# Causal attention with exact maxima and a routed feed-forward: products of 64-row head pairs, two-bank maxima, two PSUM rings and a planned TensorE order

## The reference

```
h = layernorm(x) * (1 + ca) + sa
q, k, v = h @ Wq, h @ Wk, h @ Wv          # 16 heads of 8
q, k = rope(q), rope(k)
scores = q k^T / sqrt(8), causal
x = x + ga * (softmax(scores) v) @ Wo
h = layernorm(x) * (1 + cb) + sb
x = x + gb * moe(h)                       # 8 experts, top 2, capacity 640, gelu, 128 -> 512 -> 128
```

## Time and profile before

| | |
|---|---|
| median of 3 runs | 691.77 us (690.76 to 692.2) |
| span of the profiled execution | 684.6 us; its time outside the span was not recorded, against the median it is 7.2 us |
| TensorE busy | 564.4 us, 82% |
| VectorE busy | 449.5 us, 66% |
| ScalarE busy | 350.3 us, 51% |
| GpSimd busy | 207.4 us, 30% |

### The profile page before, as it was taken

How to read it: one execution, slowest core, us unless ns; L and a number is a source line. 1 busy time by engine, 2 the same in 40 slices (tenths; PEclk the granted TensorE clock), 3 DMA queues, 4 the chain that set the end, 5 groups by cost and what they waited for, 6 DMA issues and landing times.

```text
span 684.6 us, 10732 instructions
## 1 busy us (share of the span) xinstructions
PE 564.4 (82%) x3592; PEld 249.6 (36%) x3592; DVE 449.5 (66%) x1004; ACT 350.3 (51%) x736; POOL 207.4 (30%) x501
## 2 busy tenths in 40 slices
PE   3164878899998999989999999899988841999980
PEld 2042433344332333333333334233321131687770
DVE  3866889698899898989898988898700061112123
ACT  1200424567666765747677767577788710223220
POOL 6203424512314823025202013034020224055461
PEclk9676999999999999999999999999999975799995
DMA  8830805541140611100000000000000002022206
GB/s 192 224 52 3 179 11 139 142 128 38 45 125 13 193 36 44 30 20 29 5 1 3 1 2 1 1 17 17 1 3 1 0 1 70 1 71 64 65 35 192
DMA packets 43523, 37.63 MB, mean 55 GB/s; under 512 B 4880, under 2 KB 39097, under 8 KB 43436
## 3 DMA queue, kind: packets, MB, share of 16 engines
q1 hardware_dynamic: 39312, 30.64, 17.2%
q0 software_dynamic: 2448, 4.63, 1.9%
q10 hardware_dynamic: 1708, 1.67, 1.2%
HBM read 20.39 MB, written 17.05 MB: 55 GB/s over the span
## 4 chain that ended last, share of the span: by engine, by line
PE 59%; DVE 21%; DMA 6%; issue 4%; POOL 4%; ACT 3%; SPq 3%; POOLq 0%; ACTq 0%; DVEq 0%
PE av L1163 17%; PE score L1147 14%; DVE mpart L877 12%; PE work L1125 11%; PE work L1255 6%; PE av L1269 4%; ACT PRB L714 3%; PE work L1128 1%; PE work L1099 1%; SPq L423 1%; DMA k_rows<-part 1%; DMA m_rows<-mrow 1%; PE score L1269 1%; PE work L1188 1%; POOL slots_x L647 1%
## 5 line engine op out<-in xcount | busy, mean ns | idle before, releaser
L714 ACT ACTIVATE PRB<-score 128x512 f32<-128x512 f32 (+3 forms) x640 | 300.8, 540 | 161.8 <-PE score L1147 159.1
L877 DVE TENSOR_REDUCE mpart<-work 128x1 f32<-128x512 f32 (+3 forms) x560 | 339.5, 668 | 58.1 <-PE work L1125 35.0
L1125 PE MATMUL work<-KS,QP 128*128 128x512 bf16 (+3 forms) x640 | 213.0, 356 | 39.0 <-DMA QP<-q_rows 19.2
L1147 PE MATMUL score<-QP,KS 128*128 128x512 bf16 (+3 forms) x640 | 213.5, 353 | 17.4 <-DMA QP<-m_rows 8.1
L1163 PE MATMUL av<-PRB,VX 128*9 128x512 f32 (+3 forms) x1264 | 144.8, 540 | 0.0
L610 POOL TENSOR_SCALAR_AFFINE_SELECT PRB<-PRB 128x128 f32<-128x128 f32 x256 | 70.6, 294 | 176.9 <-ACT PRB L714 174.0
L1147 PEld LDWEIGHTS score<-QP,KS 128*128 128x128 bf16 x640 | 59.1, 98 | 178.1 <-ACT PRB L714 112.3
L1125 PEld LDWEIGHTS work<-KS,QP 128*128 128x128 bf16 x640 | 64.0, 100 | 93.4 <-DVE mpart L877 42.8
L756 ACT ACTIVATE QP<-work 128x640 f32<-128x640 f32 x32 | 22.5, 703 | 72.5 <-PE work L1255 72.5
L660 POOL DMA_INDIRECT parts_y<-KS,back_to x40 | 38.9, 971 | 55.0 <-DVEq L1051 45.0
L1128 PE MATMUL work<-causal,identb 128*128 128x128 bf16 x256 | 51.8, 229 | 0.0
(11 more groups left out here) (163 smaller groups left out, 359.5 us busy)
## 6 DMA issues: line engine op xcount, KB each, us to landing
q_rows<-part SPq DMA_DIRECT2D x24, 128.0 KB, 2.3
KS<-k_rows SPq DMA_DIRECT2D x16, 192.0 KB, 4.7
k_rows<-part SPq DMA_DIRECT2D x21, 128.0 KB, 2.3
slots_x<-RT SPq DMA_DIRECT2D x8, 325.0 KB, 3.6
KS<-slots_x SPq DMA_DIRECT2D x8, 325.0 KB, 3.1
W<-in_L_ffn_c_proj_dram SPq DMA_DIRECT2D x4, 512.0 KB, 5.4
CS<-in_L_ffn_c_fc_dram SPq DMA_DIRECT2D x4, 512.0 KB, 5.5
PRB<-parts_y SPq DMA_DIRECT2D x8, 256.0 KB, 4.2
```

What stands on the lines that cost most here:

```text
L714: a.activation(PRB[:, t % PR, q0:QB], SC[t % 3][:, q0:QB], ACT.Exp, scale=SCALE).then_inc(exped, 1)
L877: v.tensor_reduce(mpart[:, u % 2, cols, k0 // QB], w[:, 0:len(heads) * keys].rearrange("p (j k) -> p j k", k=keys), AX.X, ALU.max).then_in ...
L1125: last = t_.matmul(row, QP[:, h % 2, h // 2, b % 2, (i % TB) * P:(i % TB + 1) * P], KS[:, h // 2, k0:k0 + keys], start=True, stop=not ends)
L1147: t_.matmul(SC[t % 3][:, q0:QB], KS[:, h // 2, kt * P:(kt + 1) * P], QP[:, h % 2, h // 2, b % 2, q0:QB], start=True, stop=True).then_inc(s ...
```

## The change

- Scores and maxima use 64 rows. `QP` has no zeroed copies (half the size, no clearing), and a step does both heads of a pair: one product on rows 0 to 63, one on rows 64 to 127, into two different banks.
- A maxima piece is a pair of heads in two banks (for 128 and 256 keys both pairs), and one reduction reads both banks. The mask is added by two parts for each half, with rows swapped by four small DMAs, so that it too uses 64 rows at a time.
- Two rings in the place of one: `D` with two slots of two banks for what VectorE reads, `A` with the three score banks for what ScalarE reads, scores and other steps alike.
- q and qr become one step of two products and one wide VectorE product, k and kr too; two tiles are normalised by one pair of instructions.
- The order comes from `Planner`, which keeps a clock for each engine with a cost for each step and always takes the step that could start first (priorities break ties). Value products are issued for two key tiles at a time (`AVG`). Block 1 is projected before the first maxima.
- SP follows the same list: expansion at a block's k, the q of blocks 2 and 3 reloaded by SP. `empty`, `XK`, `On` and `OnT` get memory of their own, one of the two `HG` buffers moves to `PRB`.

```diff
-NW = 4
+DW = 2
+AW = 3
+D_KIND = ("mod", "q", "k", "max", "norm", "wo", "logit", "rank", "tail")
+A_KIND = ("xt", "v", "negmax", "ot", "h2t", "score")
...
+GUESS = {"xn": (0.0, 1.0, 0.2), "xt": (0.6, 0.6, 0.1), "q": (1.9, 4.5, 0.1), "k": (1.9, 2.0, 0.1), "v": (1.0, 0.6, 0.1),
...
+         "negmax": (0.2, 0.3, 5.0)}
+NEGATE = 2.5
+LAUNCH_AT = {2: 3, 3: 5}
...
+        self.plan = [("ln", 0), ("xt", 0), ("mod", 0), ("q", 0), ("k", 0), ("ln", 1), ("mod", 1)] + projections(1)[:4]
+        self.plan += [("v", 0), ("v", 1)]
...
+    def piece(self, u, n, at):
+        pairs, i, k0, keys = max_pieces(u)[n]
+        masked = k0 + keys == P * (i + 1)
+        self.d_step(("max", u, n), at, len(pairs) * (keys / 2200 + 0.03 + 0.13 * masked), 0.13 + 2 * len(pairs) * keys / 960)
...
+    def scores(self, u, kt, a, at):
+        wide = QB - first_column(u, kt)
+        self.pe = at + wide / 2200 + 0.04
+        for half in range(2):
+            self.a_bank(0.18 + wide / 1200)
...
+    def avs(self, group, at):
+        self.pe = at + 0.2
+        for u, kt in group:
+            self.pe += (QB - first_column(u, kt)) / 610
...
+                lead = u + n / len(max_pieces(u)) - (scores[0][0] + scores[0][1] / (TB * (units()[scores[0][0]][0] + 1)) if scores else 0)
+                choices.append((self.d_start(), (-1 if lead < LEAD else 2) if self.dve - self.pe < 1.0 else 4, "max", None))
...
+                    waiting = self.a_start(2, ready)
+                    choices.append((waiting, 0 if self.act - self.pe < 0.8 else 3, "score", None))
...
+                    if waiting is not None and waiting < at + long and self.act < at + long + SLACK:
+                        at = max(at, waiting + 0.01)
+                    choices.append((at, 3.5, "av", None))
+            at, _, what, chain = min(choices, key=lambda c: (c[0], c[1]))
...
+AVG = 2
+SLACK = 0.5
+LEAD = 1.5
...
-        QP = sb("QP", [P, 2, NPAIR, 2, QB], bf16)
+        QP = sb("QP", [P, NPAIR, 2, QB], bf16)
...
+            for s in plan:
+                if s[0] == "k":
+                    expand(s[1])
+                    if s[1] == 0:
+                        swap_masks()
+                elif s[0] == "negmax":
+                    put_negmax(s[1])
...
+                        reload_q(b + 2, st.tile[u, kt, GH - 1])
...
+                        v.tensor_reduce(part[:, :, pairs[0], i % TB], w[:, :, 0:keys], AX.X,
+                                        ALU.max).then_inc(slot_free(s), 1)
...
+                        for half in range(2):
+                            rows = slice(64 * half, 64 * half + ROWS)
+                            last = t_.matmul(w[:, half, n * keys:(n + 1) * keys],
+                                             QP[rows, 2 * g + a, b % 2, (i % TB) * P:(i % TB + 1) * P],
+                                             KS[rows, 2 * g + a, k0:k0 + keys], start=True, stop=not ends)
...
+                        for part in range(2 if ends else 0):
+                            for half in range(2):
+                                rows = slice(64 * half, 64 * half + 64)
+                                last = t_.matmul(w[:, half, (n + 1) * keys - P:(n + 1) * keys], mask_i[rows, part, :],
+                                                 mask_c[rows, part, :], start=False, stop=part == 1)
...
+                    banks = [take_bank(s, half) for half in range(2)]
+                    for half, (w, ok) in enumerate(banks):
+                        rows = slice(64 * half, 64 * half + KROWS)
+                        t_.matmul(w[:, q0:QB], KS[rows, 2 * g + a, kt * P:(kt + 1) * P],
+                                  QP[rows, 2 * g + a, b % 2, q0:QB], start=True, stop=True).then_inc(ok, 1)
```

More of the change, by code:

```diff
@@ L186 @@
+AVG = 2
+SLACK = 0.5
+LEAD = 1.5
 class Steps:
     def __init__(self):
-        self.plan = make_plan()
-        self.ring = {s: n for n, s in enumerate(x for x in self.plan if x[0] not in RINGLESS)}
-        self.tile = {}
+        self.plan = Planner().run()
+        self.dring = {s: n for n, s in enumerate(x for x in self.plan if x[0] in D_KIND)}
+        self.aring, self.areads, self.tile, self.diag = {}, {}, {}, {}
+        self.bank_use = []
         for s in self.plan:
-            if s[0] == "score":
-                self.tile[s[1:]] = len(self.tile)
@@ L196, in __init__ @@
-        self.diag = {}
-        for s in self.plan:
-            if s[0] == "score" and s[2] >= TB * units()[s[1]][0]:
-                self.diag[s[1:]] = len(self.diag) + 1
+            if s[0] not in A_KIND:
+                continue
+            self.aring[s] = len(self.bank_use)
+            if s[0] != "score":
+                self.areads[s] = len(self.areads) + 1
+                self.bank_use.append(("read", self.areads[s]))
+                continue
+            _, u, kt, a = s
+            for half in range(2):
+                j = 2 * a + half
+                self.tile[u, kt, j] = len(self.tile)
+                self.bank_use.append(("exp", len(self.tile)))
+                if kt >= TB * units()[u][0]:
+                    self.diag[u, kt, j] = len(self.diag) + 1
@@ L326, in block_kernel @@
         modt_ok, modb_ok = sem("modt_ok"), sem("modb_ok")
-        full = [sem(f"full{i}") for i in range(NW)]
-        free = [sem(f"free{i}") for i in range(NW)]
+        d_full, d_free = [sem(f"d_full{i}") for i in range(DW)], [sem(f"d_free{i}") for i in range(DW)]
+        a_full, a_read = [sem(f"a_full{i}") for i in range(AW)], sem("a_read")
         roped, kparts_ok, qparts_ok = (
@@ L1121, in _ @@
                     ends = k0 + keys == P * (i + 1)
-                    for n, j in enumerate(heads):
-                        h = GH * g + j
-                        row = w[:, n * keys:(n + 1) * keys]
-                        last = t_.matmul(row, QP[:, h % 2, h // 2, b % 2, (i % TB) * P:(i % TB + 1) * P],
-                                         KS[:, h // 2, k0:k0 + keys], start=True, stop=not ends)
-                        if ends:
-                            last = t_.matmul(row[:, keys - P:keys], identb[:, :], causal[:, :],
-                                             start=False, stop=True)
@@ L1240, in turn @@
                 last.then_inc(xbt_ps, 1)
[L1242 to L1243 removed]
+            for r in range(len(dring) - DW, len(dring)):
+                pe.wait_ge(d_free[r % DW], r // DW + 1)
+            for r in range(len(st.bank_use) - AW, len(st.bank_use)):
+                wait_bank(pe, r)
             pe.wait_ge(w1_in, 16 * E // 2)
```

521 lines of the change are left out of this document (291 added, 230 removed).

## The result

The changed kernel takes 801.80 us (median of 4 runs, 799.71 to 803.69) where the kernel before takes 691.26 on the same chip: a ratio of 1.160, 95% interval 1.157 to 1.163. The forecast was 648. The span of the traced execution is 798.0 us, against 684.6 before. In every run where both were recorded, the time is about 2 us more than the span, so the trace of before is of an execution some 5 us faster than its median: marks are compared with it to within 5 us. Where executions of one kernel lie apart, a table's time is the median of all, and the marks are those of the one that was traced.

What follows compares the result with a forecast made beforehand. TensorE bounds the kernel, VectorE close behind; after, VectorE and buffers. Maxima end at 43 + 352 + 44 + 20 = 459, then 45.2, 33.7 and 103.7: span 641.6, plus 7.2 gives 649, rounded to 648; 8-in-10 range 612 to 684.

Steps and rivals of the forecast that it cites:

- Pairs run side by side: TensorE's scores and maxima: a 512-column pair of 64-row products takes 0.25 us, between bounds of 0.22 and 0.43.
- pairs don't overlap: Rival: TensorE's 64-row products run one after the other, its work is 426 us; time 692 to 706, chance 0.08.
- Reductions: VectorE's maxima: 288 two-bank reductions, mean near 1.22 us, sum 309 us by count, near 320 expected in the profile.
- The start: Block 1 projected before the first maxima: first reduction at 43 us instead of 37.7, first score at 67 as now.
- SP's stalls: Maxima rows queue behind block expansions and q reloads in SP's queue: 20 us of VectorE idleness, range 0 to 40.
- The 7.2 us outside the span: Time outside the profiled span, 691.8 - 684.6, added to the forecast span of 641.6.
- each of 80 groups costs VectorE 0.55 us: Each group of value products delays refills, idling VectorE between 0 and 0.8 us; 0.55 taken, 44 us in all.
- 44 + 20: VectorE's idleness until the maxima end: 44 us beside value-product groups plus 20 at SP's queue, 64 in all.
- two key tiles take 4.9 us: ScalarE's exponentials: 3.9 + 1.0 us per two key tiles, exactly the present 2.44 per key tile.
- 45.2 as now: From the end of the maxima to the last value products: 45.2 us, unchanged because the 2.44 us period stays.
- The clock: Rival: TensorE idles enough to fall to 1.2 GHz; with a third of the stage cold, about 700 us, chance 0.04.
- three signs named for being wrong: Pairs starting 0.4 us apart, the lower clock in the stretch, or a few maxima-row stalls of 5 us or more.

Runs made afterwards that it cites:

- e3: The changed kernel with value products in groups of one key tile instead of two, the planner ordering anew: 743.6 us, ratio 1.073.
- e4: The changed kernel, but a score pair computes into its first bank before waiting for the second, instead of claiming both first: 756.6 us, ratio 1.092.
- e5: The changed kernel with both edits, value products in groups of one key tile and a pair's banks claimed one by one: 729.1 us, ratio 1.051.
- e15: The kernel before, old order, with two slots of two banks for all ring steps, two-bank maxima, products still on 128 rows: 713.6 us, ratio 1.039.
- e17: The kernel before, old order, with every single-head score and maxima product, and the masks of those pieces, on 64 rows: 704.1 us, ratio 1.019.
- e2: The changed kernel with one extra 128-row product, later overwritten, before each score pair, after its banks are taken: 883.3 us, ratio 1.275.
- e8: The kernel before, old order, with every single-head score and maxima product on its head's 64 rows, masks still on 128: 721.9 us, ratio 1.041.
- e6: The changed kernel with four narrow products of zeros into the open value bank before each score pair's wait for banks: 782.8 us, ratio 1.129.
- e9: The changed kernel with one extra 64-row product, later overwritten, into a pair's first bank before the wait for the second: 773.5 us, ratio 1.113.
- e14: The changed kernel with value products in groups of one and two extra 64-row products before the wait for a pair's second bank: 750.7 us, ratio 1.094.
- e16: The kernel before, old order, with value products of two key tiles issued together as a group of 16: 692.0 us, ratio 1.002.
- e18: The kernel before, old order, with the edits of e16 and e17 together: 741.9 us, ratio 1.075.
- e11: e5 with SP putting unit 0's maxima row ahead of block 1's expansion: 709.2 and 727.2 us in two executions.
- e12: e5 with the planner's costs for a score's exponential and a reduction set as the trace shows them: 712.0 and 731.1 us in two executions.
- e13: Changed kernel, groups of one, one extra 64-row product before a pair's second-bank wait, maxima rows moved from SP's to GpSimd's queue: 729.0 us, ratio 1.062.

## Why the prediction was wrong

The sizes of the single parts were right. Pairs run side by side: 0.22 us forecast at the lower bound, 0.25 taken, 0.22 measured. The rival "pairs don't overlap" is out. Reductions: 288, mean of the wide ones 1.219 us (1.22 forecast), 322 us in all (320). The start: first reduction at 45.3 (43), first exponential at 73.7 (67 for its score, 72.98 measured). SP's stalls: VectorE idle 13.1 us before 74.2 and 8.7 before 118.4, TensorE's queue standing at a score whose maxima row was late; 22 us, 20 forecast. Epilogue and experts take 3.4 us longer. The 7.2 us outside the span were about 2, the rest being the faster execution that was traced; as before and forecast were treated alike, this does not touch the 648. One sum beside the forecast is off: 0.28 us a pair makes TensorE's work 334 us, not 328.

**The step that each of 80 groups costs VectorE 0.55 us, together 44, failed.** The last maxima row comes at 577, not 459. Of the 118 us, 2 are the later start, 13 VectorE's busy time (364.6 against 352) and 103 idleness: 167 us where the sum had 44 + 20. I had costed a group at 1.83 us, its time at full clock, counted one refill behind it, and let a pair take its banks when they came. In fact the pair's claim needs two of three banks free at once, and the group was 3.5 us long whenever the clock was low. The waits show it: the forecast had VectorE's idleness "in pieces under 1 us", and the largest entry has 47 pieces of 1.6 us in the mean, up to 3.9, such as the 3.14 us behind the group at 395.94. e3, e4 and e5 put 58, 45 and together 73 us on these two grains. e15, at full clock, shows a second term that the sum lacked: the two-bank slots of VectorE's ring, 3.9% by themselves in the old order.

**The step on ScalarE's side, that two key tiles take 4.9 us (the present 2.44 each), failed, and with it "45.2 as now".** It held with banks claimed singly, groups of one and a high clock (2.43 in e5). As changed it is 7.7: 3.5 for a group at the lower clock, 1.44 and twice 1.21 for the pairs (two exponentials need 1.0) and 0.3 to the next group. The tail behind unit 15 is 79.6 us instead of 45.2, of which some 7 are the score work moved behind the mark.

**The clock, a rival at 0.04, was weighed wrongly.** The lower clock was one of the three signs named for being wrong, and it came. I expected TensorE about 80% busy at a clock near 1.00, from a stretch that was 84% busy at 1.00. It was 78% busy and granted 0.81; in the last unit 68% and 0.66; e17 had 92% and 0.90. So one row of 128-row products said little about a mix with 64-row ones and other pauses. It was priced too low as well: about 700 us in the prediction, where the kernel took 802. My own count should have warned: 318 us of work in the 461 from 43 to 504 is 69%, and only busy time, which reads 464 where I counted 420, made it look like 80. With the low clock, TensorE's busy time over the whole stage (45 to 656 us) is 453 us, about what it was (464 from 37.5 to 547). In busy time nearly all that the 64 rows took away came back: value products went from 144.8 to 188.6 us at half as many groups, and a pair that stands alone counts 0.39 us though the next can start after 0.22. The Trainium skill (TensorE: Matmul & The Clock Gate, A second HAM failure mode: psum-queue depth-cycling) describes just this, a TensorE that pauses often between groups of matmuls while it cycles through PSUM banks and moves between its two clock levels; the traces agree, with 0.81 at pauses of 0.6 us before the pairs. Such pauses did not always bring the lower level: from 404 to 412 us the changed kernel has similar ones (0.47 to 0.62) at a granted 1.00, and its groups take 1.90.

The rule that changing the tiling mode drains the array (the Trainium skill, TensorEngine Tiling (Array Packing), Key Properties) was left out of the sum. e2 and e8 agree with it at 0.08 to 0.12 us a change; in the changed kernel the masks are on 64 rows, so it explains little of the loss.

**How much of it is the clock?** Some 20 us at least: e6's fillers, which leave the distance of the pairs as it was, give back 19, and e9's give back 28. At the other end e14 is nearly at full clock and still 9.4% above before, but with filler in the way. The effects overlap: a coarser grain makes longer pauses, these lower the clock, and a low clock makes the grain coarser still (e16, e17 and e18 cost 1, 13 and 44 to 51 us, more together than the sum). A split that adds up can't be given.

**What stays open.** e5's 31.5 us before unit 5: block 1 projected ahead of the maxima and rows put behind expansions belong there, but e11, e12 and e13 moved waits about without a clear gain. TensorE is granted 0.72 from 45 to 174 us in e5 and 0.89 from 45 to 143 us before, so the clock has a part there too, of unknown size. I did not run the planner's order with 128-row products, nor the changed kernel with four single banks for VectorE's ring, nor a plan that gives the expansions another time.

## What to carry to other kernels

When a change takes work off the bounding engine until no engine is full, the sum of busy times no longer predicts the end. Price each block by what it keeps others from doing while it runs or waits, above all claims on several buffers at once, and prefer the finer grain even where the coarse one saves overhead. When a change makes TensorE idle more often in a stage than the rows of before show it, price the stage at both clock levels and give the lower one a serious chance: here pauses, clock and group length seem to feed each other. Try each part alone in the old order first: here the three parts cost 0.2 (not told from nothing), 1.9 and 3.9%, and none was a gain.

## What the runs showed of the hardware

- Two 64-row products of 512 columns, on rows 0 to 63 and 64 to 127, into two banks, start 0.01 us apart (e8: 380.27 and 380.28), and the next two can start 0.22 later (changed kernel, above): the full factor of two.
- Changing between 128-row and 64-row products costs 0.08 to 0.12 us each way (e2: a start 0.31 after the last instead of 0.22; e8: 0.30 instead of 0.22, and back 0.17 instead of 0.05).
- One reduction over 1,024 elements in two banks takes 1.22 us, two over 512 in a row about 1.28 (0.68 for one, 1.88 for three).
- A TensorE with 92% of its time busy was granted 0.88 to 0.90 where many products used 64 rows (e8, e17), and 1.00 at 90 to 93% where all used 128 (e15). The runs don't tell whether the rows or the pattern of the pauses does that.
- Products that nobody needs made the kernel 19 us faster with the pairs no closer together (e6, clock 0.81 to 0.88), and up to 28 (e9).
- The granted clock can fall just as a long group begins: 0.50 from 396 to 399 us in the changed kernel, and 16 value products take 3.56 us instead of 1.83.
- A 12 KB put to memory takes 7 to 9 us while an expansion's transfers are in flight, from SP's queue as from GpSimd's; alone it is followed by its gets after 1.4.
